# A two-layer attention kernel: the order of one queue's transposes

## The reference

```
xn = layernorm(x) * w + b
q  = softmax(xn @ Wq + bq)            # over each head's features
k  = softmax(xn @ Wk + bk, masked)    # over the 512 tokens
v  = (xn @ Wv + bv), masked
att = k^T v   per head                 # 64x64 or 32x32
y   = q att   per head
scale, shift = split(silu(emb) @ W_emb + b_emb)
h   = layernorm(y) * (1 + scale) + shift
out = x + silu(h) @ W_out + b_out
```

## Time and profile before

| | |
|---|---|
| median of 3 runs | 808.76 us (807.19 to 809.26) |
| profiled execution, its own time | 809.02 us |
| its span, first to last instruction | 807.2 us |
| TensorE busy in the span | 764.1 us, 95% |
| VectorE, ScalarE, GpSimd busy | 87%, 64%, 54% |
| SP's DMA queue, share of the 16 DMA engines | 69.0% |
| mean granted TensorE clock | 0.989 |

### The profile page before, as it was taken

The page is one execution under the profiler, slowest core; times in us unless marked ns, Lnnn a source line. Parts: engine busy times, 40 slices in busy tenths (PEclk is TensorE's granted clock), DMA queues, the critical chain, the costliest instruction groups (busy, mean ns, idle before and its releaser), DMA issues.

```text
span 807.2 us, 16864 instructions
## 1 busy us (share of the span) xinstructions
PE 764.1 (95%) x6359; PEld 370.6 (46%) x6359; DVE 698.4 (87%) x1427; ACT 517.5 (64%) x1011; POOL 438.6 (54%) x433
## 2 busy tenths in 40 slices
PE   5997979999999999999999999999999999999986
PEld 2444434354454445444454544444454544444442
DVE  6899967798998999999978899888888899888885
ACT  5896763856758687686866685565657476560723
POOL 2475573553856658487564655547265545544352
PEclk9998989999999999999999999999999999999999
DMA  9956497764957859596594939688584939477552
GB/s 329 322 108 187 116 264 215 141 146 130 184 167 138 168 152 184 170 180 174 112 180 122 191 109 178 169 153 200 94 195 115 183 122 184 116 139 150 83 127 79
DMA packets 291249, 130.73 MB, mean 162 GB/s; under 512 B 261440, under 2 KB 261824, under 8 KB 291168
## 3 DMA queue, kind: packets, MB, share of 16 engines
q1 hardware_dynamic: 288432, 125.27, 69.0%
q10 hardware_dynamic: 2736, 4.39, 1.6%
HBM read 47.74 MB, written 16.88 MB: 80 GB/s over the span
## 4 chain that ended last, share of the span: by engine, by line
PE 74%; DVE 14%; issue 4%; ACT 4%; DMA 2%; POOL 1%; SPq 0%; DVEq 0%; ACTq 0%; POOLq 0%
PE ring L535 66%; PE ring L710 3%; PE att_ps L659 2%; DVE sb_k_or_qt L1043 2%; DMA sb_ht_parts<-sb_htok 2%; ACT sb_k_or_qt L1435 1%; DVE sb_q_sum L1102 1%; DVE sb_row_peak L882 1%; DVE sb_ht_parts L1156 1%; DVE ring L1128 1%; DVE sb_y_stats L1132 1%; DVE sb_x L1118 1%; ACT sb_v_or_q L1482 1%; ACT sb_v_parts L1484 1%; DVE ring L1073 1%
## 5 line engine op out<-in xcount | busy, mean ns | idle before, releaser
L535 PE MATMUL ring<-sb_w_hi,sb_xt_parts 128*128 128x512 f16 x1024 | 309.0, 379 | 0.0
L535 PE MATMUL ring<-sb_w_lo,sb_xt_parts 128*128 128x512 f16 x512 | 194.0, 379 | 0.0
L535 PE MATMUL ring<-sb_w_hi,sb_ht_parts 128*128 128x512 f16 x512 | 157.2, 382 | 10.1 <-DMA sb_ht_parts<-sb_htok 6.0
L535 PEld LDWEIGHTS ring<-sb_w_hi,sb_xt_parts 128*128 128x128 f16 x1024 | 100.5, 98 | 126.0 <-issue 6.6
L535 PE MATMUL ring<-sb_xt_parts,sb_w_hi 128*128 128x512 f16 x496 | 150.1, 385 | 7.8 <-issue 7.3
L1693 POOL TENSOR_TENSOR sb_htok<-sb_ht_parts,sb_htok 128x512 f16<-128x512 f32 x60 | 75.0, 1272 | 136.7 <-ACT sb_htok L1468 136.7
L1709 POOL TENSOR_TENSOR sb_tanh<-sb_v_or_q,sb_kq_hi 128x512 f16<-128x512 f32 x64 | 74.1, 1158 | 88.1 <-ACT sb_kq_hi L1499 87.3
L535 PE MATMUL ring<-sb_w_lo,sb_ht_parts 128*128 128x512 f16 x256 | 97.8, 382 | 0.0
L535 PE MATMUL ring<-sb_xt_parts,sb_w_lo 128*128 128x512 f16 x248 | 95.0, 383 | 0.0
L1492 ACT ACTIVATE sb_v_or_q<-ring,sb_ln_one 128x512 f32<-128x512 f32 x64 | 44.0, 687 | 61.4 <-DVE ring L1078 60.4
L535 PEld LDWEIGHTS ring<-sb_w_hi,sb_ht_parts 128*128 128x128 f16 x512 | 50.4, 99 | 70.9 <-issue 9.0
(11 more groups left out here) (232 smaller groups left out, 1398.6 us busy)
## 6 DMA issues: line engine op xcount, KB each, us to landing
out<-sb_x SPq DMA_DIRECT2D x14, 1024.0 KB, 4.8
sb_rows_now<-film_rows SPq DMA_DIRECT2D x16, 512.0 KB, 4.6
sb_x<-out SPq DMA_DIRECT2D x8, 1024.0 KB, 5.3
sb_x<-in_x SPq DMA_DIRECT2D x7, 1024.0 KB, 6.7
sb_mask_add<-mask_terms SPq DMA_DIRECT2D x15, 256.0 KB, 5.7
sb_w_hi<-in_L_cond_W_emb SPq DMA_DIRECT2D x1, 1536.0 KB, 14.1
sb_w_lo<-in_L_cond_W_emb SPq DMA_DIRECT2D x1, 1536.0 KB, 14.3
sb_w_hi<-in_L_cond_film_emb_W ACTq DMA_DIRECT2D x1, 1536.0 KB, 11.8
```

The costliest lines, as they stand in the source:

```text
L535: last = nc.tensor.matmul(out, lhs, rhs, start=(n == 0), stop=(n == len(pairs) - 1))
```

## The change

In SP's order the second half of x is turned directly behind its first half, ahead of the queries. The queries are turned in two halves (tiles 0 and 1, then 2 and 3), each high and low, so four transposes of 8 blocks stand where two of 16 stood, with a semaphore for each half of each part. Y waits for the second half's semaphores only before its third tile. Outside units 3 to 5 the film table is loaded behind the keys' transposes and ahead of h's. In unit 0 the queries go ahead of both halves of x. The readers of kq_hi and of the low part wait for both halves.

```diff
-        kt_hi_ready, kt_lo_ready, qt_hi_ready, qt_lo_ready = (
-            sem("kt_hi_ready"), sem("kt_lo_ready"), sem("qt_hi_ready"), sem("qt_lo_ready"))
+        kt_hi_ready, kt_lo_ready = sem("kt_hi_ready"), sem("kt_lo_ready")
+
+        qt_hi_ready, qt_lo_ready = ([sem(f"{name}{j}") for j in range(2)] for name in ("qt_hi_ready", "qt_lo_ready"))
...
-            def turn_q(u):
-                sp.wait_ge(kt_hi_ready, 16 * (u + 1))
-                sp.wait_ge(kt_lo_ready, 16 * (u + 1))
-                turn(blocks_of(qt_hi), kq_hi[:], q_hi_ready, 4 * (u + 1), qt_hi_ready)
-                turn(blocks_of(qt_lo), q_lo, q_lo_ready, 4 * (u + 1), qt_lo_ready)
+            def turn_q(u, j):
+
+                if j == 0:
+                    sp.wait_ge(kt_hi_ready, 16 * (u + 1))
+                    sp.wait_ge(kt_lo_ready, 16 * (u + 1))
+                at = slice(2 * j * D, 2 * (j + 1) * D)
+                turn(blocks_of(qt_hi[:, at]), kq_hi[:, at], q_hi_ready, 4 * u + 2 * j + 2, qt_hi_ready[j])
+                turn(blocks_of(qt_lo[:, at]), q_lo[:, at], q_lo_ready, 4 * u + 2 * j + 2, qt_lo_ready[j])
...
                 turn_k(0)
+                turn_q(0, 0)
+                turn_q(0, 1)
                 turn_x(0, 0)
-                turn_q(0)
                 turn_x(0, 1)
...
                 turn_k(u)
+                if not PREP <= u < PREP + 3:
+                    sp.wait_ge(z_ready, 4 * u)
+                    load_rows(u)
                 turn_h(u)
...
-                sp.wait_ge(z_ready, 4 * u)
                 if PREP <= u < PREP + 3:
+                    sp.wait_ge(z_ready, 4 * u)
                     sp.wait_ge(shift_summed, 3 + u - PREP + 1)
-                load_rows(u)
+                    load_rows(u)
                 if u < LAST:
                     turn_x(u, 0)
-                turn_q(u)
+                    turn_x(u, 1)
+                turn_q(u, 0)
+                turn_q(u, 1)
                 if u < LAST:
-                    turn_x(u, 1)
...
             def attend(u, between=lambda t: None):
-                pe.wait_ge(qt_hi_ready, 16 * (u + 1))
-                pe.wait_ge(qt_lo_ready, 16 * (u + 1))
                 if u not in Q_FIRST:
                     pe.wait_ge(att_lo_ready, att_count(u))
                 for t in range(T):
                     if t % 2 == 0:
+                        pe.wait_ge(qt_hi_ready[t // 2], 16 * (u + 1))
+                        pe.wait_ge(qt_lo_ready[t // 2], 16 * (u + 1))
                         take_bank("Y", t, u)
...
                 if u:
-                    act.wait_ge(qt_hi_ready, 16 * u)
+                    for j in range(2):
+                        act.wait_ge(qt_hi_ready[j], 16 * u)
...
                 elif unit == LAST:
-                    act.wait_ge(qt_lo_ready, 16 * UNITS)
+                    for j in range(2):
+                        act.wait_ge(qt_lo_ready[j], 16 * UNITS)
```

## The result

The changed kernel takes 815.43 us (median of 6 runs, 813.10 to 816.45), the kernel before 809.07 (6 runs, 807.19 to 809.98) beside it: ratio 1.0076, 95% interval 1.0061 to 1.0091. It is slower by 6.4 us, where the prediction had it 4 us faster and ended its range at 808.8. The profiled execution took 814.56 us, its span is 812.8.

The account below looks back on a forecast made before the run. TensorE was taken as the bound, idle mainly before K, waiting for x's second half. K gaps and clock +8.0, last unit +1.1, queries -0.6, h -2.0, unit 6 -1.4, unit 1 -1.0: gain 4.1, 804.6 us, range 800.9 to 808.8.

Parts of the forecast that it names:

- the 44.95 counted: Units 7 to 14: forecast length of a unit in us, 44.85 of undisturbed TensorE work and 0.1 of joints.
- the 8.0 forecast: Units 7 to 14: gain in us from closing the gaps before K, including 1.66 of clock in unit 7.
- 0.25 a unit: Before O in units 7 to 14: TensorE's expected wait for h in us, 2.0 in all, bounds 0 and 7.
- rival 2: The wait moves to O: closing K's gaps gives DVE's waits only; gain 1.8, 807.2 us, chance 0.18.
- The queue's last landing moves forward by the filled hole, some 2.1 us in unit 10: SP's queue: x's second half fills SP's 2.15 us standstill before the queries, so the last landing comes that much sooner.
- So it is just in time: Y, unit 10: queries' second half lands at 553.6, needed at 553.5; waits of 0.6 us over eight units.
- rival 3: The queries come late: four short transposes take 7.2 us instead of 5.2, Y waits; gain 0.5, 808.5 us, chance 0.08.
- So h's transposes move back by 0.6 if the table starts as soon as the keys are through: Between keys and h: the table's 1.3 us transfer meets 0.7 us of still DMA engines, delaying h by 0.6 us.
- the relief counted on: h's landing: 4.8 to 6.4 us after issue; without the table close behind, half of these 1.6 comes back.
- Rival 4: The table blocks h: h waits for the table's landing, 1.9 us a unit instead of 0.6; 814.7 us, chance 0.11.
- rivals 1: All of it: the table fits into the still time, losses shrink to 1.0; gain 8.1, 800.9 us, chance 0.13.
- the trace disagrees and decides: Before unit 7's K: the 1.98 us gap cost 1.66 us of clock, against the skill's rule of under about 3 us.

Follow-up runs that it names:

- experiment 3: The changed kernel with the film table issued ahead of the keys' transposes instead of ahead of h's: 805.64 us, ratio 0.9954.
- experiment 5: The changed kernel with the film table ahead of the keys' transposes and x's second half behind the queries, so halves only: 804.26 us, ratio 0.9938.
- experiment 4: The kernel before with only the film table moved, ahead of the keys' transposes: 809.04 us, ratio 1.0004.
- experiment 1: The changed kernel with the film table back behind h: 813.58 us, ratio 1.0059.
- experiment 9: The kernel before with only x's second half moved directly behind its first, queries whole, table behind h: 813.51 us, ratio 1.0056.
- experiment 2: The kernel before with only the film table moved, ahead of h: 813.19 us, ratio 1.0051.
- experiment 10: The kernel before with only the queries turned in halves, x's second half last, table behind h: 807.15 us, ratio 0.9980.
- experiment 7: The changed kernel with the table ahead of the keys and the halves of x and the queries interleaved: 805.69 us, ratio 0.9952.
- experiment 12: The changed kernel with x's second half behind the queries, so halves only, table still ahead of h: 813.36 us, ratio 1.0055.

## Why the prediction was wrong

**What bounds the kernel: right, but for unit 7.** K waited for x's second half, and in the changed kernel it starts right behind Y in every unit; units 8 and 11 last 44.80, below the 44.95 counted. The closed gaps before K gave 6.8 us (6.3 of standing, and 0.07 eight times, by which two stages overlap where nothing parts them) and the clock its 1.7, but unit 7's K, V and Q lost 1.0 of that again: 7.5 for the 8.0 forecast.

Unit 7 was to give the most, 1.98 and the clock's 1.66, and gave nothing: from the end of unit 6's Y to the end of its own it takes 48.49 us in the kernel before, 48.78 in the changed one, 48.34 and 48.10 in experiments 3 and 5. h's first transpose is issued 27.9 us after the end of unit 6's Y in the kernel before and in experiments 3 and 5 alike, whether K starts 1.98 later or at once. So there the work on DVE and behind it counts from Y, and TensorE, once it comes sooner, waits for it in K and before O. The prediction had seen this chain in unit 10 and counted 0.25 a unit for it, unit 7 included; what happens there is rival 2's mechanism, in one unit.

The last unit gave 0.6 for 1.1. The gap before its K is closed, but from K to the end it lasts 0.7 longer, and in it the clock fell where it had not in the kernel before (last section). That the one comes from the other is not shown.

**The step that failed first: "The queue's last landing moves forward by the filled hole, some 2.1 us in unit 10".** It took SP's idle time for idle time of the transfers. The window of the hole has a DMA share of 0.81 (experiment 4), so by an estimate only 0.19 of 2.15, 0.4 us, was free. From the issue of h's first transpose to the queue's last landing the kernel before takes 21.4 us (mean of the eight units), the changed one 20.6 and experiment 1 20.8: 0.6 to 0.8 forward, not 2.1. Two transposes of x now stand in front of the queries, 3.4 us on average from their first issue to the queries' first, so the queries' last landing went back by 2.0 (43.2 to 45.2). "So it is just in time" was therefore wrong by 1.2. Waits inside Y cost 3.1 in the eight units less 0.6 before Y, against 0.6 forecast, and 1.93 in unit 1, where nothing was counted. Experiments 1 and 9 show this step alone: it turns the change into a loss before the table comes into it. It is near rival 3 in its effect, but not by rival 3's mechanism: the four short transposes were issued in 1.23 to 1.27 each in unit 10, 1.34 on average in the eight. Here the prediction was right that two more transposes cost no 2 us each: the four landings of unit 10's queries lie 1.3 apart. The 2 us of the Trainium skill, "DMA: Bandwidth & Descriptors", section "Anatomy of one DMA", are given there for DMAs on GpSimd's path, and these are SP's.

**The table ahead of h: mechanism right, size too small.** The forecast took "So h's transposes move back by 0.6 if the table starts as soon as the keys are through". In the eight units the time from h's first issue to its pair's landing grew from 7.8 to 8.8. The table's issue came as early as forecast, 2.3 behind that of the low keys (536.77 against 534.51), and h's first part was issued as soon as it was ready, in both kernels; but its pair then held SP for 7.18 instead of 5.17. And the relief counted on, half of 1.6, did not come: without the table behind it h's pair lands 7.6 after its issue (experiment 3), 0.2 sooner than before. Waits before O are 5.9 in the eight units against 2.0 forecast (bounds 0 and 7). 2.57 of them are unit 7's, and with the table ahead of the keys unit 7 still waits 1.47 of 1.7 in all (experiment 3), so some 4.2 are the table's.

Unit 6 lost 1.5 against 1.4, which is luck: the queries were to be 0.8 late there and cost nothing, and the wait before O grew from 0.52 to 2.36. By the end of unit 1's Y 2.8 were lost against 1.0: 2.1 in Y, 1.7 before O, less 1.0 ahead of these, 0.7 of it because the clock fell in unit 0's Y now and not in unit 1's K. The wait before O is 7.66 for the 5.97 of the earlier trace rows (TensorE's timeline):

```profile
115.34 0.58 PE L544 MATMUL ring<-sb_w_hi,sb_ht_parts 128*128 128x512 f16 x1 [7.66 <-DMA sb_ht_parts<-sb_htok]
```

Units 3 to 5, counted at nothing, lost 0.7, inside unit 5's Y.

**The sum.** Forecast +8.0 +1.1 -0.6 -2.0 -1.4 -1.0 = 4.1. Measured by the two profiles: +7.5 +0.6 -2.5 -5.9 -1.5 -2.8 -0.7 = -5.3, against -5.6 between the spans. Rival 4, at 814.7, had the time nearly right, in part by luck, and half of the reason: it blamed the table alone, which experiment 2 puts at 4.2, while x's place costs 4.9 by experiment 9; and it kept the whole gain and charged O with 10 where it cost 5.9. With the 1.4 that the halves gain the single edits make 7.7, not the 6.4 measured. The two delays cover each other in part: from experiment 1 to the changed kernel, which differ in the table's place alone, the waits before O of units 7 to 14 grow from 0 to 5.9 and those in and before Y shrink from 9.0 to 3.1, while the queries land at the same time, 45.0 and 45.2. A wait for h before O also moves Y towards them.

**The chances.** The forecast and rivals 1 and 2 all took the filled hole as given. A rival in which it is not, with everything else the same, was missing.

## What to carry to other kernels

Before counting an issuer's hole as time to be won, look at the DMA share in that window: a queue that has been handed its work is busy while the issuer waits. For a serial queue write down for each member its landing and the latest time at which it is needed, and keep them in the order of need; moving the one that ends last forward pays only if what it passes has more slack than its own length. Closing a gap of the bounding engine gives back only as much as the next chain allows: ask from which event each of its later inputs counts (unit 7). And a bulk transfer belongs where the queue waits for a producer anyway (here ahead of the keys' transposes), not into its full stretch; two edits can be worth 1.4 and nothing alone (experiments 10 and 4) and 4.7 together (5).

## What the runs showed of the hardware

**A gap's length does not tell whether the clock falls.** The prediction took 1.66 us for a clock at 0.53 behind a gap of 1.98. In the run with halves only, table behind h, the gap at the same place was 2.18, and the clock stayed at 1.00, the 2.4 GHz level, in the 3.6 us behind it (windows):

```profile
371.81:375.41 3.60, 3.60 (x17) 1.65 (x18) 3.49 (x10) 2.83 (x8) 0.73 (x2) 1.00 0.48 183
```

Behind the gaps of 2.36 and 2.57 of the changed kernel and 3.23 of experiment 2 the 48 matmuls of O took 10.52 and 10.53, full speed too. But behind 1.92 in experiment 7 and 3.09 in experiment 12, at the same place as the 2.36 and the 3.23, before unit 6's O, the granted clock was 0.50, the 1.2 GHz level, at first, and the 48 took 12.22 (experiment 12, the chain):

```profile
357.93 3.09 issue
361.02 12.22 PE ring L544 x48
```

The closest pair is in the last unit, in front of Y: 2.20 in the kernel before and the clock stayed up, 2.21 in the changed one and it fell to 0.50 soon behind it (at 784.7; of the 48 matmuls of O behind that Y the first 24 took 6.5 us by TensorE's timeline where they had taken 5.35; here the chain):

```profile
785.82 6.45 PE ring L544 x24
```

In both cases of the gap before unit 7 the engine had run Y's 96 small matmuls just before. The Trainium skill, "TensorE: Matmul & The Clock Gate", section "Why this matters for your kernels", asks for gaps under about 3 us; 2.18, 2.36, 2.57 and 3.09 agree with it, 3.23 did no harm although it is longer, and 1.98, 1.92 and 2.21 did although they are shorter. Executions of one kernel differ too: the mean granted clock of the kernel before lies between 0.986 and 0.996 in 24 of them. So "the trace disagrees and decides" rested on one gap, and what decides stays open; such a price should enter a sum as a bound, not as a term, and two profiles should be compared only after a look at where the clock fell in each.

**Transposes move fewer bytes than a broadcast in the same time.** In experiment 1, in a window that holds the queries' four transposes and next to nothing else (share and GB/s at the end), the DMA engines are 94% busy at 185 GB/s; the table went at 417.

```profile
550.76:558.00 7.24, 6.12 (x73) 2.98 (x71) 4.31 (x8) 2.72 (x9) 4.79 (x5) 1.00 0.94 185
```

The Trainium skill, "Advanced Engine Details and Errata", section "X-Bar Transpose (TRN2)", expects 350 to 400 GB/s of them; here it is about half. That is why the hole and the table mattered: at 1.3 us for 8 blocks, the twelve such lengths of h, x and queries take some 16 us (an estimate) of the about 20 between h's issue and the last time that Y can bear.
